# Mixture-of-experts stage of a gated two-layer kernel: gate and up computed with the weights held in the array and the rows run through, no transposes of the hidden rows, down one step earlier

## What is computed

```python
x = x + tanh(g_xattn[0]) * L0_xattn(layernorm(x), ctx, ctx)          # causal attention, 16 heads of 32
x = x + tanh(g_ffn[0])   * L0_ffn(layernorm(x), gate_w, w_gate, w_up, w_down)   # experts
x = x + tanh(g_xattn[1]) * L1_xattn(layernorm(x), ctx, ...)          # two attentions, projections
x = x + tanh(g_ffn[1])   * L1_ffn(layernorm(x), weight, bias)        # ternary weights
```

```python
g = xg @ w_gate[e]; u = xg @ w_up[e]     # 512 -> 192 each
y = (silu(g) * u) @ w_down[e]            # 192 -> 512
```

## Time and profile before

| | |
|---|---|
| time, median of 3 runs | 1506.52 us (1506.15 to 1506.72) |
| the profiled execution, its own time | 1510.09 us |
| its span, first to last instruction | 1508.3 us |
| granted TensorE clock, mean | 0.972 of full |
| span in which TensorE is busy | 89% |
| VectorE, ScalarE, GpSimd busy | 64%, 61%, 34% |

### The profile page before, as it was taken

How to read it: one execution, slowest core, us unless ns; L and a number is a source line. 1 busy time by engine, 2 the same in 40 slices (tenths; PEclk the granted TensorE clock), 3 DMA queues, 4 the chain that set the end, 5 groups by cost and what they waited for, 6 DMA issues and landing times.

```text
span 1508.3 us, 37766 instructions
## 1 busy us (share of the span) xinstructions
PE 1338.1 (89%) x11005; PEld 841.2 (56%) x11006; DVE 970.1 (64%) x2389; ACT 920.8 (61%) x2261; POOL 520.3 (34%) x532
## 2 busy tenths in 40 slices
PE   4888888958989999999999999677989898898987
PEld 3665555634656666666666666344555555565553
DVE  6888888754645555655655632254777776877764
ACT  4777777724656666665666666335766667566663
POOL 1044444555333433332000001665554544442000
PEclk8999999969999999999999999988999999999999
DMA  2044434459888767767676545776655645543000
GB/s 73 29 175 186 152 147 148 163 208 321 280 289 280 264 224 248 242 221 240 220 242 223 183 146 146 138 110 87 102 82 82 105 59 98 95 69 69 1 15 28
DMA packets 96149, 233.42 MB, mean 155 GB/s; under 512 B 11824, under 2 KB 11824, under 8 KB 91440
## 3 DMA queue, kind: packets, MB, share of 16 engines
q0 software_dynamic: 33712, 113.79, 30.2%
q1 hardware_dynamic: 62336, 118.34, 23.7%
HBM read 140.84 MB, written 91.24 MB: 154 GB/s over the span
## 4 chain that ended last, share of the span: by engine, by line
PE 44%; DMA 9%; DVE 8%; issue 7%; POOL 3%; ACT 3%; SPq 3%; DVEq 0%; ACTq 0%; POOLq 0%
PE bank L1329 17%; PE bank L1353 9%; PE bank L1586 6%; DMA xs<-y_tiles,slot_ix 5%; PE bank L1317 4%; DMA x_slots<-blank 2%; PE bank L277 2%; POOL xs L449 2%; PE bank L1340 1%; PE bank L297 1%; PE bank L1592 1%; DVE l_nmax L344 1%; ACT l_probs L312 1%; PE bank L259 1%; DVE l_stack L398 1%
## 5 line engine op out<-in xcount | busy, mean ns | idle before, releaser
L1329 PE MATMUL bank<-wh,xT 128*128 x1280 | 340.7, 328 | 4.1 <-DVE hp L1445 2.7
L449 POOL DMA_INDIRECT xs<-y_tiles,slot_ix x120 | 192.7, 1606 | 237.3 <-DMA y_tiles<-ysb 99.8
L312 ACT ACTIVATE l_probs<-bank,l_bias 128x256 f32<-128x256 f32 (+1 forms) x512 | 225.5, 452 | 68.9 <-DVE l_bias L346 68.3
L1329 PE MATMUL bank<-wl,xT 128*128 x640 | 209.9, 328 | 0.0
L344 DVE TENSOR_REDUCE l_nmax<-bank 128x2 f32<-128x512 f32 (+1 forms) x256 | 158.3, 619 | 67.7 <-PE bank L259 38.6
L1435 DVE SCALAR_TENSOR_TENSOR hv<-bank,sg 128x192 f32<-128x192 f32 x160 | 57.0, 356 | 224.1 <-ACT sg L1389 201.3
L324 ACT ACTIVATE l_probsT<-bank 128x512 f32<-128x512 f32 (+1 forms) x256 | 141.0, 551 | 69.8 <-PE bank L297 69.4
L1404 ACT ACTIVATE ysb<-bank,xg 128x512 f32<-128x512 f32 x160 | 110.0, 687 | 118.1 <-PE bank L1353 117.8
L1383 ACT ACTIVATE xT<-bank 128x1024 f16<-128x1024 f16 x160 | 162.6, 1017 | 15.5 <-PE bank L1317 15.3
L1329 PEld LDWEIGHTS bank<-wh,xT 128*128 128x128 f16 x1280 | 125.8, 98 | 80.2 <-issue 9.6
L1353 PE MATMUL bank<-wh,hT 128*128 x480 | 156.0, 379 | 1.4 <-ACT hT L1396 1.4
(11 more groups left out here) (249 smaller groups left out, 2589.6 us busy)
## 6 DMA issues: line engine op xcount, KB each, us to landing
xg<-x_slots SPq DMA_DIRECT2D x160, 272.0 KB, 2.8
y_tiles<-ysb SPq DMA_DIRECT2D x160, 256.0 KB, 2.4
raw<-in_experts_dram POOLq DMA_DIRECT2D x30, 1280.0 KB, 6.7
x_slots<-blank SPq DMA_DIRECT2D x33, 272.0 KB, 4.1
xs<-in_x_dram SPq DMA_DIRECT2D x8, 512.0 KB, 4.9
cbuf<-in_ctx_dram SPq DMA_DIRECT2D x8, 512.0 KB, 6.4
stage<-in_mats_dram POOLq DMA_DIRECT2D x4, 1024.0 KB, 8.3
room<-in_ctx_dram SPq DMA_DIRECT2D x8, 512.0 KB, 5.1
```

Source lines behind the costliest of these rows:

```text
L312: last = self.nc.scalar.activation(self.probs[:, s % 2, u, 0:nk], self.pS[s % 2][:, u * S : u * S + nk], ACT.Exp, bias=self.bias[:, s % 4, ...
L449: return nc.gpsimd.indirect_dma_start(to, None, self.y_tiles[0 : (MT + 1 - k) * P, :], ix, compute_op=ALU.add)
L1329: last = nc.tensor.matmul(bGU[t.place % 2][:, 0:GU], xT[:, t.place % 2, xo + c * P : xo + (c + 1) * P], wp[:, bass.ds(w, 1), c * GU : (c + ...
```

## The change

`gate_up` swaps the operands. The weights are stationary, in blocks of 128 columns, and the tile's 128 rows (`xT`) run through: 3 blocks m by 4 chunks c by 3 passes, 36 matmuls with 128 columns. The order of the passes puts the two with the same weights next to each other. The result comes out turned: hidden numbers on the partitions, rows on the free axis. For this the host arranges an expert's columns as gate 0:128, gate 128:192 with up 128:192, up 0:128. `turn_h`, `copy_h`, `hp` and their semaphores go; VectorE writes the parts straight to `hT` in six instructions, of which two take 64 partitions alone and move them between the halves. `down` follows two steps after `gate_up`, not three. `silu_of` takes 256 columns, not 192. VectorE's `hidden(t)` now waits for `y_ps` (the `down` of tile t-2 has read `hT`) where it waited for `ht_ps`. TensorE's table `t_pe` holds the expert of tile t-2 in the place of that of t-3.

```diff
-            chain.mark(v.tensor_copy(plan.t_pe[:, 0:3], row_e[:, 0:3]))
-            chain.mark(v.scalar_tensor_tensor(plan.t_pe[:, 3:MT], row_e[:, 0 : MT - 3], float(E), row_e[:, 3:MT], ALU.mult, ALU.add))
+            chain.mark(v.tensor_copy(plan.t_pe[:, 0:2], row_e[:, 0:2]))
+            chain.mark(v.scalar_tensor_tensor(plan.t_pe[:, 2:MT], row_e[:, 0 : MT - 2], float(E), row_e[:, 2:MT], ALU.mult, ALU.add))
...
-                passes = [(0, wh), (0, wl), (H, wh)]
-                for c in range(HC):
-                    for k, (xo, wp) in enumerate(passes):
-                        last = nc.tensor.matmul(bGU[t.place % 2][:, 0:GU], xT[:, t.place % 2, xo + c * P : xo + (c + 1) * P],
-                                                wp[:, bass.ds(w, 1), c * GU : (c + 1) * GU].rearrange("p a w -> p (a w)"),
-                                                start=c == 0 and k == 0, stop=c == HC - 1 and k == 2)
+                passes = [(0, wh), (H, wh), (0, wl)]
+                for m in range(3):
+                    for c in range(HC):
+                        at = c * GU + m * P
+                        for k, (xo, wp) in enumerate(passes):
+                            last = nc.tensor.matmul(bGU[t.place % 2][:, m * P : (m + 1) * P],
+                                                    wp[:, bass.ds(w, 1), at : at + P].rearrange("p a w -> p (a w)"),
+                                                    xT[:, t.place % 2, xo + c * P : xo + (c + 1) * P],
+                                                    start=c == 0 and k == 0, stop=c == HC - 1 and k == 2)
                 last.then_inc(gu_ps, 1)
 
-            def turn_h(t):
+            def down(t, e):
+                w = e & (NW - 1)
                 pe.wait_ge(h_ready, t.n + 1)
                 if t.at(-2).exists():
-                    pe.wait_ge(ht_ready, t.n - 1)
-                o = bHT[t.place % 2][:, :].bitcast(F16)
-                for c in range(3):
-                    last = nc.tensor.transpose(o[:, c * P : (c + 1) * P], hp[:, t.place % 2, c * P : (c + 1) * P], id16[:])
-                last.then_inc(ht_ps, 1)
-
-            def down(t, e):
-                w = e & (NW - 1)
-                pe.wait_ge(ht_ready, t.n + 1)
-                if t.at(-2).exists():
                     pe.wait_ge(y_ready, t.n - 1)
-                hi, lo, rest = (hT[:, t.place % 2, c * P : (c + 1) * P] for c in range(3))
+                hi, rest, lo = (hT[:, t.place % 2, c * P : (c + 1) * P] for c in range(3))
...
                 gate_up(t, e)
                 if t.at(-2).exists():
-                    turn_h(t.at(-2))
-                if t.at(-3).exists():
-                    down(t.at(-3), before)
+                    down(t.at(-2), before)
...
-                    act.wait_ge(h_made, t.n - 1)
-                nc.scalar.activation(sg[:, t.place % 2, :], bGU[t.place % 2][:, 0:FI], ACT.Silu, scale=1.0 / (SC_N * SC_W))\
+                    act.wait_ge(h_made, 2 * t.n - 2)
+                nc.scalar.activation(sg[:, t.place % 2, :], bGU[t.place % 2][:, 0 : 2 * P], ACT.Silu, scale=1.0 / (SC_N * SC_W))\
...
-                if t.at(-2).exists():
-                    copy_h(t.at(-2))
...
-                v.scalar_tensor_tensor(hv[:, :], bGU[t.place % 2][:, FI:GU], SC_H / (SC_N * SC_W), sg[:, t.place % 2, :],
+                if t.at(-2).exists():
+                    dve.wait_ge(y_ps, t.n)
+                gu, silus, out, half = bGU[t.place % 2], sg[:, t.place % 2, :], hT[:, t.place % 2, :], FI - P
+                unscale = SC_H / (SC_N * SC_W)
+                v.scalar_tensor_tensor(hv[:, 0:P], gu[:, 2 * P : 3 * P], unscale, silus[:, 0:P], ALU.mult, ALU.mult).then_inc(h_made, 1)
+                v.scalar_tensor_tensor(hv[0:half, P : 2 * P], gu[half:P, P : 2 * P], unscale, silus[0:half, P : 2 * P],
                                        ALU.mult, ALU.mult).then_inc(h_made, 1)
...
+                dve.wait_ge(h_made, 2 * t.n + 2)
+                v.tensor_copy(out[:, 0 : 2 * P], hv[:, :]).then_inc(h_hi, 1)
+                dve.wait_ge(h_hi, t.n + 1)
+                v.tensor_tensor(out[:, 2 * P : 3 * P], hv[:, 0:P], out[:, 0:P], ALU.subtract)
+                v.tensor_tensor(out[half:P, P : 2 * P], hv[0:half, P : 2 * P], out[0:half, P : 2 * P], ALU.subtract).then_inc(h_ready, 1)
```

More of the change, by code:

```diff
@@ L1158, in experts @@
         xT = sb("xT", [P, 2, 2 * H], F16)
-        sg = sb("sg", [P, 2, FI])
-        hv = sb("hv", [P, FI])
-        hp = sb("hp", [P, 2, 2 * FI], F16)
+        sg = sb("sg", [P, 2, 2 * P])
+        hv = sb("hv", [P, 2 * P])
         hT = sb("hT", [P, 2, 3 * P], F16)
@@ L1171, in experts @@
         gu_ps, silu, h_made, h_hi, h_ready = sem("gu_ps"), sem("silu"), sem("h_made"), sem("h_hi"), sem("h_ready")
-        ht_ps, ht_ready, y_ps, y_ready = sem("ht_ps"), sem("ht_ready"), sem("y_ps"), sem("y_ready")
+        hv_clear, y_ps, y_ready = sem("hv_clear"), sem("y_ps"), sem("y_ready")
         block = es.enter_context(nc.Block(no_gpsimd_drain=True))
@@ L1371, in _ @@
             last = Tile(MT - 1, (MT - 1) % 8, (MT - 1) // 8)
-            turn_h(last.at(-1))
-            turn_h(last)
-            for t in (last.at(-2), last.at(-1), last):
+            for t in (last.at(-1), last):
                 down(t, pe.value_load(t_e[0:1, t.column()]))
@@ L1387, in silu_of @@
                 if t.at(-2).exists():
-                    act.wait_ge(h_made, t.n - 1)
-                nc.scalar.activation(sg[:, t.place % 2, :], bGU[t.place % 2][:, 0:FI], ACT.Silu, scale=1.0 / (SC_N * SC_W))\
+                    act.wait_ge(h_made, 2 * t.n - 2)
+                nc.scalar.activation(sg[:, t.place % 2, :], bGU[t.place % 2][:, 0 : 2 * P], ACT.Silu, scale=1.0 / (SC_N * SC_W))\
                   .then_inc(silu, 1)
-            def copy_h(t):
-                act.wait_ge(ht_ps, t.n + 1)
-                if t.at(-2).exists():
-                    act.wait_ge(y_ps, t.n)
-                nc.scalar.activation(hT[:, t.place % 2, :], bHT[t.place % 2][:, :].bitcast(F16)[:, 0 : 3 * P], ACT.Copy)\
-                  .then_inc(ht_ready, 1)
             def weigh(t):
@@ L1420, in _ @@
             last = Tile(MT - 1, (MT - 1) % 8, (MT - 1) // 8)
-            copy_h(last.at(-1))
             weigh(last.at(-2))
-            copy_h(last)
             weigh(last.at(-1))
@@ L1434, in hidden @@
                     dve.wait_ge(h_ready, t.n)
-                v.scalar_tensor_tensor(hv[:, :], bGU[t.place % 2][:, FI:GU], SC_H / (SC_N * SC_W), sg[:, t.place % 2, :],
-                                       ALU.mult, ALU.mult).then_inc(h_made, 1)
[L1437 to L1445, removed]
+                if t.at(-2).exists():
[4 more added lines that the diff above has]
+                v.scalar_tensor_tensor(hv[0:half, P : 2 * P], gu[half:P, P : 2 * P], unscale, silus[0:half, P : 2 * P],
+                                       ALU.mult, ALU.mult).then_inc(h_made, 1)
+                dve.wait_ge(h_made, 2 * t.n + 2)
[3 more added lines that the diff above has]
+                v.tensor_tensor(out[half:P, P : 2 * P], hv[0:half, P : 2 * P], out[0:half, P : 2 * P], ALU.subtract).then_inc(h_ready, 1)
+            v.memset(hv[FI - P : P, P : 2 * P], 0.0).then_inc(hv_clear, 1)
+            dve.wait_ge(hv_clear, 1)
             LATE = 3 * WEXP // 10
@@ L2004, in arrange @@
     wg, wu, wd = f["L0_ffn_w_gate"], f["L0_ffn_w_up"], f["L0_ffn_w_down"]
-    gu = np.concatenate([wg.reshape(E, HC, P, FI), wu.reshape(E, HC, P, FI)], axis=3)
+    wg, wu = wg.reshape(E, HC, P, FI), wu.reshape(E, HC, P, FI)
+    gu = np.concatenate([wg[..., :P], wg[..., P:], wu[..., P:], wu[..., :P]], axis=3)
     gu = gu.transpose(0, 2, 1, 3).reshape(E, P, HC * GU)
```

## The result

| | before | after |
|---|---|---|
| time, median | 1506.62 us | 1693.66 us (1689.31 to 1695.21, 4 runs) |
| ratio | | 1.1199, 95% interval 1.1156 to 1.1242 |
| the profiled execution, its own time / its span | 1510.09 / 1508.3 us | 1689.31 / 1687.4 us |
| a step of `experts`, mean of 159 | 3.77 us | 4.92 us |

The change makes the kernel 12% slower; 1684 us was forecast for the median, and 1688 for a profiled execution that took 1510.1 before. Two executions further down stand far outside the rest and are left out of the ratios: 2609.64 us of the kernel with the fixed block, beside three of 1533 to 1549, and 1620.07 us of the kernel before, beside 18 of 1505 to 1518.

What follows compares the result with a forecast made beforehand. TensorE's array bounds the kernel now, its sequencer after: 3.77 to 4.9 us a step, over 159 steps 180 us, less some 2, is +178: 1688 us profiled, 1684 median. Range 1630 to 1730, a little under 8 in 10.

Steps and rivals of the forecast that it cites:

- The bound moves from the array to its sequencer: TensorE in `experts`: sequencer's step grows to 4.9 us, over the array's 3.55, so the array waits for its instructions.
- The price of an operation: TensorE's sequencer: each register operation costs 0.117 us; 16 more in `gate_up` add 1.87 us a step.
- the knee: Point where the sequencer overtakes the array: up to 5 more register operations a tile, the step stays array-bound.
- the bounds 0.10 to 0.125: Range in us for one register operation, giving 1.60 to 2.00 us a step for the 16 added in `gate_up`.
- one step without waits: TensorE's step from 744.0 to 747.0, 3.0 us; less the table's load of 0.30, 2.7 us by 23 is 0.117.
- the 5.15 of the upper end: Longest forecast step of `experts` in us, from a free step of 3.17 plus 2.00 for the added operations.
- The sum: Whole kernel: 1.13 us a step over 159 steps is 180 us, less some 2 for start-up waits: +178.
- The array's -0.10: TensorE's array a tile: `gate_up` +0.07 us, `turn_h` -0.17, so 3.55 us instead of 3.64.
- Costed at nothing: ScalarE, VectorE, the new wait of `hidden(t)`, later `down` and SyncE: all hidden by a step of 4.9 us, so 0.
- the deadline of `split`: VectorE: `split`'s late part ends 7.8 us after `gate_up(t)` ends; `gate_up(t+3)`, which wants it, starts at 11.8.
- The rival that would have been faster: TensorE's sequencer does not grow, through folded addresses or loads taking them differently; array sets the pace, 1492 us; chance 0.09.
- The 0.13 of waits: Waits and start-up a tile on TensorE before, added by the faster rival to the array's 3.55: 3.68 us.

Runs made afterwards that it cites:

- the kernel with the fixed block: Changed kernel with all 36 weight loads of `gate_up` reading one fixed block (the identity), not the expert's weights: 1532.77, 1535.12 and 1548.56 us, ratio 1.0206.
- The nearest form of the change: Changed kernel with all `gate_up` weight loads from one fixed block (the identity) and four buffers of `hT` instead of two: 1516.15 us, ratio 1.0042.
- four written-out bodies: Changed kernel with `gate_up` written as four branches, one per place of the weights, so addresses are constants, and four buffers of `hT`: 1933.86 us, ratio 1.2781.

## Why the prediction was right

**The bound moves from the array to its sequencer.** Right. 25 operations against 9, as counted; step 4.92 us against 4.9; waits put down to "issue"; pairs 0.080 apart; loads still 98 ns; the clock at 1.00. The runs turn the correlation into a cause: with 22 of the 25 operations gone and the same pairs, the time falls from 1694 to 1542; with 16 operations added to the old form, it rises to 1720 (one execution).

**The price of an operation.** Predicted 0.117, measured 0.119 beyond the knee and 0.118 or more with the pairs equal; the bounds 0.10 to 0.125 held it. It came from one step without waits, divided by its 23 operations and waits as if all cost the same, and with the pairs priced at nothing. That a wait costs what an operation costs is shown by no run, so some luck is in how close it came. A slip in the sum changed nothing: 3.17 + 2.00 is 5.17, not the 5.15 of the upper end.

**The sum.** 1688 for the profiled execution, which took 1689.3. The median of four is 1693.7, 9.7 above the forecast 1684: I carried the 3.6 us by which the profiled run of before lay above its median over to a kernel whose profiled run lies 4.4 below it. That is the runs' own spread, not a term.

**The array's -0.10.** Right, and worth nothing: undisturbed steps with the fixed block are 3.5 us (0.44 + 36 x 0.056 + 1.08), against 3.64. The Trainium skill's 81 ns for a sustained matmul of 128 columns ("TensorE: Matmul & The Clock Gate", Back-to-back issue gap) is not what the array needs here: 56 ns in a row of 36. It is close to what the changed kernel shows, 80 ns, but for another reason, the register operations between the pairs.

**Costed at nothing.** Right at this step length (four buffers of `hT`: 1.1193 against 1.1199), with its condition stated. But the cover was thinner than I wrote. I counted six instructions, as in the list of the change; `hidden` has five and takes 1.6 us, not 2.2. And I gave the deadline of `split` with a step of 4.9 only, and left out the `hidden(t+1)` behind it, for which `gate_up(t+3)` waits. The fixed block's timeline shows it:

```profile
714.78 2.17 PE L1330 MATMUL bank<-xT,id 128*128 128x128 f16 x36
716.79 0.38 PE L1346 MATMUL bank<-wh,hT 128*128 x1
...
724.94 0.61 PE L1316 MATMUL bank<-id,xg 128*128 128x128 f16 x8
727.22 2.17 PE L1330 MATMUL bank<-xT,id 128*128 128x128 f16 x36 [1.67 <-DVE hT L1424]
```

```profile
718.17 0.29 DVE L1417 SCALAR_TENSOR_TENSOR hv<-bank,sg 128x128 f32<-128x128 f32 x1 [1.97 <-PE bank L1346]
...
720.19 1.49 DVE L1439 TENSOR_SCALAR wh<-raw  x1 [0.45 <-issue]
721.81 0.96 DVE L1442 SCALAR_TENSOR_TENSOR wl<-raw,wh  x1
723.45 2.03 DVE L1442 SCALAR_TENSOR_TENSOR wl<-raw,wh  x1 [0.68 <-issue]
...
726.79 0.28 DVE L1424 TENSOR_TENSOR hT<-hv,hT 64x128 f16<-64x128 f32 x1
```

`gate_up(t)` ends its starts at 716.8, where `down` begins. `hidden(t)` starts 1.4 behind that, `hidden(t+1)` ends 10.3 behind it, and `gate_up(t+3)` was due at 725.4, 8.6 behind: late by 1.7 here, by 47.1/31 = 1.5 on average. Of these 10.3 us, 1.3 are gaps around the pieces of `split`, which the sum did not have. At 4.9 a step the due time is 11.8, so with the same 10.3 the cover holds by 1.5 us, not by the 4.0 that the sum gave `split`.

**The rival that would have been faster.** Its condition is false, 16 operations were really added, and its price was wrong too: not 1492 but 1542 us (with 3 operations; 1533 to 1549 with none). The step of that rival that failed is "the array would set the pace: 3.55 + 0.13". The 0.13 of waits was taken over from before, while `hidden`, which now waits for `down(t-2)` and is 0.4 us longer, would have been late for each expert. So the change loses, by 2%, even where its addresses are nearly free, unless `hT` has more buffers.

No version here beats the kernel before. The nearest form of the change, at a ratio of 1.0042, leaves out the weights' addresses altogether, and with them the product with the gate and up weights.

## What to carry to other kernels

Price a reordering of matmuls on the sequencer as well as on the array: count the distinct addresses that depend on a register, multiply by the price of an operation read from a step without waits, and compare the sum with the array's. Swapping which operand is stationary keeps the columns but can multiply the addresses: here three blocks of 128 columns took the place of one of 384, and 24 addresses that of 8. And when one bound is removed, sum the others again at the new pace: the waiting for `hidden` that costs nothing in steps of 4.9 us was 47 us in steps of 3.55.

## What the runs showed of the hardware

- A register operation on TensorE's sequencer takes 0.118 to 0.119 us of its time, although the record says 32 to 46 ns: 0.119 from 8 to 16 operations more in the old form, at least 0.118 from 14 to 25 in the new one, where the pairs are equal. Dealing out 12 more pairs of load and matmul under the array's pace cost 0.02 us a step.
- A computed address costs about the same for the stationary as for the moving operand (these two prices), and its load is still issued ahead (95 to 98 ns, pairs 0.056 apart with 3 operations a tile).
- In a loop with four written-out bodies a step, one branch took up to 5.2 us, and 307 packets of instructions were fetched where the changed kernel has 61.
- The VectorE copy of 128x256 f32 to f16 took 0.42 us out of a PSUM bank and 0.29 us out of `hv` in SBUF.
